# One comparison for a unit's destination one-hots in the third pass of a graph kernel

## The reference

```python
msg = x[src] @ W.T + b                                   # passes 1 and 2
summed = segment_sum(msg, dst);  out = summed / max(cnt, 1)
...
et = edge_emb_W[edge_type]                               # pass 3
m = relu(concatenate([x[src], et]) @ msg_W.T + msg_b)
agg = segment_sum(m, dst) / clip(deg, 1)
h = x + (agg @ upd_W.T + upd_b)
return layernorm(h) * ln_g + ln_b                        # x is added once more outside
```

## Time and profile before

| what | value |
|---|---|
| median of 3 runs | 1761.03 us (1753.79 to 1761.88) |
| time of the profiled execution | 1756.86 us |
| its span in the trace | 1755.1 us |
| third pass in it, first gather to the end | 1147 to 1755 us |
| busy in the whole span: PE, DVE, POOL | 1536.7, 1255.8, 1115.6 us |
| line 2299 | 676 instructions, 212.7 us busy |

### The profile page before, as it was taken

How to read it: one execution, slowest core, us unless ns; L and a number is a source line. 1 busy time by engine, 2 the same in 40 slices (tenths; PEclk the granted TensorE clock), 3 DMA queues, 4 the chain that set the end, 5 groups by cost and what they waited for, 6 DMA issues and landing times.

```text
span 1755.1 us, 37837 instructions
## 1 busy us (share of the span) xinstructions
PE 1536.7 (88%) x14583; PEld 1269.1 (72%) x14583; DVE 1255.8 (72%) x3039; ACT 559.5 (32%) x807; POOL 1115.6 (64%) x1154
## 2 busy tenths in 40 slices
PE   0188988899988898789999999679999999999996
PEld 0177877778777777545555556578998999999995
DVE  7889888998999886401323423367788988898886
ACT  3545444454445443400101211222222322232322
POOL 3466464646556462677777777367777777777772
PEclk9899999999999999989999999779999999999998
DMA  4344344434444344588787888655556565565552
GB/s 130 129 139 151 130 148 138 142 139 143 151 146 148 131 141 150 190 265 245 232 273 244 274 272 244 205 159 180 182 178 187 183 183 182 182 184 179 184 173 79
DMA packets 179056, 312.12 MB, mean 178 GB/s; under 512 B 28611, under 2 KB 123413, under 8 KB 178869
## 3 DMA queue, kind: packets, MB, share of 16 engines
q1 hardware_dynamic: 137910, 225.66, 38.5%
q0 software_dynamic: 40960, 83.95, 17.1%
HBM read 228.39 MB, written 81.11 MB: 176 GB/s over the span
## 4 chain that ended last, share of the span: by engine, by line
PE 48%; DVE 24%; POOL 13%; issue 9%; DMA 3%; DVEq 2%; ACT 1%; SPq 0%; POOLq 0%
PE banks L1250 47%; POOL rows L916 13%; DVE region_b L1753 4%; DVE region_b L1732 3%; DVE region_a L1732 3%; DVE src_hot L1732 2%; DVE src_in_all L1732 1%; DVE hot L1732 1%; DMA region_a<-near_tab 1%; DVEq L2235 1%; DVE region_b L1758 1%; DMA rows<-table,src_all 1%; DVE rank L1769 1%; DVE region_b L1766 1%; DVEq L1827 1%
## 5 line engine op out<-in xcount | busy, mean ns | idle before, releaser
L916 POOL DMA_INDIRECT rows<-table,src_all x992 | 1046.1, 1055 | 518.6 <-issue 311.2
L1250 PE MATMUL banks<-region_a,htab 128*128 128x256 bf16 (+1 forms) x4128 | 643.0, 307 | 13.5 <-issue 11.1
L1250 PEld LDWEIGHTS banks<-region_a,htab 128*128 128x128 bf16 (+1 forms) x4128 | 406.9, 99 | 183.5 <-issue 18.0
L1200 ACT ACTIVATE region_a<-banks 128x1024 bf16<-128x1024 f32 (+2 forms) x272 | 234.4, 863 | 325.6 <-PE banks L1250 325.6
L1250 PE MATMUL banks<-region_a 128*128 128x256 f32 (+1 forms) x1896 | 330.2, 322 | 0.0
L1250 PEld LDWEIGHTS banks<-region_a 128*128 128x128 f32 (+1 forms) x1896 | 263.4, 161 | 33.0 <-issue 3.6
L2243 DVE TENSOR_TENSOR agg<-agg,banks 128x128 f32 (+1 forms) x171 | 54.6, 319 | 284.8 <-PE banks L1250 222.1
L1250 PE MATMUL banks<-hot,rows 128*128 128x128 bf16 (+1 forms) x2560 | 213.0, 239 | 13.9 <-DMA rows<-table,src_all 10.1
L1250 PEld LDWEIGHTS banks<-hot,rows 128*128 128x128 bf16 (+1 forms) x2560 | 204.5, 130 | 24.3 <-issue 17.5
L2299 DVE TENSOR_SCALAR region_a<-columns,slot_dst 128x256 f32<-128x256 f32 x676 | 212.7, 381 | 0.0
L1250 PE MATMUL banks<-type_rows,region_b 128*128 128x128 bf16 x1092 | 179.8, 221 | 0.3 <-DVE region_b L2159 0.3
(11 more groups left out here) (226 smaller groups left out, 1592.3 us busy)
## 6 DMA issues: line engine op xcount, KB each, us to landing
region_a<-near_tab SPq DMA_DIRECT2D x100, 384.0 KB, 4.4
near_tab<-region_a SPq DMA_DIRECT2D x68, 448.0 KB
region_b<-in_etype SPq DMA_DIRECT2D x52, 512.0 KB, 5.4
near_tab<-region_a SPq DMA_DIRECT2D x68, 384.0 KB
region_a<-near_tab SPq DMA_DIRECT2D x32, 512.0 KB, 6.2
rows<-table,src_all POOLq DMA_INDIRECT x992
src_in_all<-src_tab SPq DMA_DIRECT2D x52, 224.0 KB
region_b<-type_tab SPq DMA_DIRECT2D x52, 224.0 KB
```

What stands on the lines that cost most here:

```text
L916: nc.gpsimd.indirect_dma_start(out=to[:, c, :], out_offset=None, in_=tab[layer], in_offset=bass.IndirectOffsetOnAxis(ap=cols[:, c:c + 1], ...
L1200: nc.scalar.activation(near[slot][:, at:at + own, :], near_ps[h][:, 0:own, :], ACT.Copy)\
L1250: return nc.tensor.matmul(to, left, right, start=start, stop=stop)
```

## The change

`destination_hot(u)` compares all buckets of a unit at once. In place of 7 (or 6) `tensor_scalar` instructions, each with 256 columns and its bucket's destinations as the per-partition scalar, there is one `tensor_tensor` of 7 x 256 = 1792 (or 1536) columns. Its first input is `columns1`, repeated for each bucket by a step of zero (`every`). Its second is the unit's own columns of `slot_dst`, each repeated 256 times by a step of zero. Output, order, waits and the semaphore at the end are as they were.

```diff
 def destination_hot(u):
     dve.wait_ge(unit_summed, c.unit(u - 2))
-    for j, t in enumerate(UNITS[u]):
-        last = V.tensor_scalar(dst_hot_f[u % 2][:, j, :], columns1[:, :],
-                               slot_dst[:, b * BUCKETS + t:b * BUCKETS + t + 1], None, ALU.is_equal)
-    last.then_inc(dst_hot_ready, 1)
+    m, own = len(UNITS[u]), slice(b * BUCKETS + UNITS[u][0], b * BUCKETS + UNITS[u][-1] + 1)
+    V.tensor_tensor(dst_hot_f[u % 2][:, 0:m, :], every(columns1, m),
+                    slot_dst[:, own].unsqueeze(2).broadcast_to([P, m, WIN_B]), ALU.is_equal)\
+        .then_inc(dst_hot_ready, 1)
```

## The result

The changed kernel takes 1858.6 us (median of 4 runs, 1855.47 to 1859.87) against 1759.3 us for the kernel before: 1.0569 times the time, 95% interval 1.0549 to 1.059. The profiled execution took 1859.08 us with a span of 1857.3 us, 102.2 us more than in the earlier trace rows. The prediction was 1855 us.

What follows compares the result with a forecast made beforehand. PE bounds the third pass's middle, POOL has 12 us of slack; holds add 119 us, less 7 removed, 12.3 slack and 1 at the tail: +98.7 us on 1756.9, say 1855 us, range 1820 to 1890.

Steps and rivals of the forecast that it cites:

- PE sets the pace before, DVE's saving is worth nothing: Third pass, middle: PE busy 444 of 448 us, so DVE's saving of about 17 us gains nothing on the path.
- Durations: Line 2299 on DVE: merged comparisons take 2.02 and 1.75 us, 196 us in all against 212.7 before.
- The hold: POOL: a gather starting inside a two-SBUF-input comparison stands still until its end, ending 0.82 us later; 119 us added.
- The mean over phases: Gathers start on average 0.62 us into a comparison as phase drifts; holds 1.28 and 1.01 us, ends 54 and 184 us.
- The gathers' mean: Line 916 on POOL: mean gather time rises to 1.29 us from 1.023.
- The stretch: POOL, first gather to end of last: grows by 99.7 us, from 575.2 to 675 us.
- POOL's slack: Third pass: POOL's 18.9 us of waits for PE, less ordinary gaps, leave 12.3 us to absorb holds.
- The rest of the sum: Tail after the last gather: line 2325 no longer waits for PE, 0 to 1.9 us back, 1 taken.
- PE's idle time: Third pass: PE idle some 100 us, waiting for ACT's line 1225 or DVE.
- the second rival: Gathers lose the change-over between DVE instructions as well: +42 us, 1897 us; chance 0.05.
- the third rival: By list order: gathers fall into step with DVE, starting late in each comparison; +34 us, 1790 us; chance 0.05.
- the fourth in its list: DVE was the true limit in the pass and its 17 us come out: 1740 us; chance 0.02.

Runs made afterwards that it cites:

- the PSUM form: Changed kernel with the merged comparison's first input read from PSUM, types of half the chunks left out: 1759.9 us, 1.0006 times the kernel before.
- eight one-input comparisons: Kernel before with line 1931's two-SBUF-input comparison made as eight one-input ones of 128 columns: 1774.9 us; with gaps ahead of lines 2159 and 2299, 1763.4 us.
- seven two-input ones: Kernel before with each of a unit's 7 or 6 comparisons made as a tensor_tensor with two SBUF inputs: 1820.3 us, 1.0349.
- the kernel with halves and a gap: Kernel before with two two-SBUF-input comparisons per unit (4 and 3 or 2 buckets), DVE waiting between them: 1796.4 us, 1.0211; slower chip 2058.9 us, 0.967.

## Why the prediction was right, point by point

- **PE sets the pace before, DVE's saving is worth nothing.** Right: removing 165 us of line 2299 gave 1.0000, and the PSUM form, which keeps the saving and drops the hold, 1.0006.
- **Durations.** 2.02 and 1.75 us predicted from line 1931 and the slope, 2.035 and 1.748 measured; 196 us of DVE predicted, 196.7 measured. The saving of 16 us is itself made by the gathers: 27 us of the old 212.7 were comparisons waiting for a gather's end, which the prediction did not see, though the mean of 381 ns stands well above the median of 341. Without these waits the old comparisons would have taken some 185 us, less than the new ones (an estimate from the two numbers).
- **The hold.** That a gather ends 0.82 us after the comparison's end was read from one row of the second pass and one of the third; 99 gathers held by line 2299 in the trace after do the same and add up to 107 us. 103 started in it in all, and their time above 0.94 us is 114 us, against 119 predicted.
- **The mean over phases was luck in part.** The prediction let the phase between the engines drift and took a start 0.62 us into the comparison. It doesn't drift: 61 of the 103 gathers started 0.50 to 0.61 us into it, in even units 46 of 52. The hold by line 1931 sets this, as in the unit shown above: the held gather ends 0.82 us after line 1931, the next starts 0.30 us later, and that is 0.53 us into the comparison. In odd units the starts lie between 0.16 and 1.21 us. The mean of all is 0.68 us. That it lies near the assumed 0.62 comes from the lengths of the instructions in between, not from phases that are spread evenly.
- **The gathers' mean.** 1.29 us predicted, 1.287 measured.
- **The stretch.** From first gather to the end of the last 675 us predicted; 1822.18 + 0.94 - 1150.88 = 672.2 us measured. POOL's slack of 12.3 us was taken up in full: no wait for PE is left, and its idle time fell by 161.1 - 148.2 = 12.9 us.
- **The rest of the sum.** The first gather came 3.8 us later than in the earlier trace rows, in passes that the change doesn't touch; the tail after the last gather is 34.2 us in place of 32.9, where I had taken 1 us off. 97.0 + 3.8 + 1.3 = 102.2 us (with rounding), the difference of the two spans. Line 2325 did not wait for PE any more at the end, but the rows came later than I had thought, since their transfers land some 3 us after POOL is done with the last gather (1826.2 against 1823.1).
- **PE's idle time.** Some 100 us predicted; from 1147 us to the end it is 710 - 611.3 = 98.7 us. But 608 - 582.1 = 25.9 us of idle time had been there before, so only 73 us are new. PE's busy time grew by 29 us for the same work, at a granted clock of 0.97 in the middle in place of 1.00. PE had room for both, since POOL set the pace.
- **What the prediction had too low** is the second rival, lost change-overs. In the changed kernel it stayed small: three gathers stood still through lines 2293 and 1931 (two before), and three went past the merged comparison to the end of line 2112 behind it (2.7 to 2.8 us each), some 5 us for the six by my estimate from their durations. But the reasoning (few such cases in the trace before) doesn't carry to kernels with runs of such instructions: there lost turns cost some 10 us (eight one-input comparisons, 1774.9 against 1763.4) to some 60 us (seven two-input ones, against what was expected).
- **A slip in the numbering.** The prediction calls DVE as the true limit "the third rival" where it speaks of fewer instructions; it is the fourth in its list.

## What to carry to other kernels

Ahead of merging vector instructions, look at which form they have and what else reads SBUF: one `tensor_tensor` with both inputs in SBUF can save the vector engine 16 us and still cost the kernel a hundred, if GpSimd issues indirect transfers beside it. Busy time of an engine off the critical path tells nothing of what it takes from its neighbour; look at the neighbour's shortest duration, its mean, and its slack, here 12 us in 575. If a long two-input instruction is needed, reading one input from PSUM took the whole loss away here (1.0006). A short gap between two such instructions gave back half of it (1.0419 to 1.0211).

## What the runs showed of the hardware that I had not expected

- A held gather can lose its turn again and again: up to seven one-input comparisons in a row behind a type comparison (3.49 us the longest gather). A gap of 0.13 us between two DVE instructions was worth 34 us of kernel time.
- It goes both ways: in the kernel before, 139 one-input comparisons of 256 columns waited for a gather and ended 0.11 us after it, up to 0.22 us late, while the gathers ran on.
- A one-input float32 comparison of 7 x 256 columns, the 7 by a step of zero, takes 2.07 us and held none of 81 gathers, one of 6 x 256 takes 1.07 us and slowed all 34. Only the number of buckets differs between the two; that the odd count is what makes the first slow was not tested with other counts.
- One chip ran the kernel before in 2125 us in place of 1759, and there the kernel with halves and a gap was faster than the kernel before (0.967) where it is slower elsewhere (1.0211). POOL waited 117 us for PE in its third pass, against 2 us in the same kernel on a chip of the usual speed, so it had more slack than its gathers lost by being held (75 us above 0.94 us each). No trace of the kernel before was taken on that chip, and why it gains there was not tested.
